# A recurrent mixer gated by a recursive top-2 expert network on one NeuronCore: a rewritten schedule

## The reference

```python
xn = layernorm(x)
# mixer: shifted input, six 128x128 projections, a scan along the sequence
xx = prev(xn) - xn
lin = lambda mix, W: (xn + xx * mix) @ W.T
r, alpha, g = sigmoid(lin(x_r, W_r)), sigmoid(lin(x_a, W_a)), sigmoid(lin(x_g, W_g))
decay = exp(-softplus(lin(x_w, W_w))); u = alpha * tanh(lin(x_k, W_k)) * lin(x_v, W_v)
state = state * decay + u                   # per time step
mixed = r * state
s = (group_norm(mixed, 16 groups of 8) * g) @ W_out.T + b_out
# experts: four rounds; round r routes with its own Wg, experts are shared
cur = xn
for r in range(4):
    cw = softmax over the top 2 of 4 logits of cur @ Wg[r] + bg[r]
    cur = cur + sum_e cw[e] * (gelu(cur @ W1[e] + b1[e]) @ W2[e] + b2[e])   # 128 -> 512 -> 128
out = x + s * silu(cur)
```

## Time and profile before

| | us |
|---|---|
| median of 3 runs | 847.47 (847.16 to 848.54) |
| the profiled execution | 848.68 |
| its span, first to last instruction | 846.8 |
| mean granted TensorE clock | 0.981 of full |

### The profile page before, as it was taken

How to read it: one execution, slowest core, us unless ns; L and a number is a source line. 1 busy time by engine, 2 the same in 40 slices (tenths; PEclk the granted TensorE clock), 3 DMA queues, 4 the chain that set the end, 5 groups by cost and what they waited for, 6 DMA issues and landing times.

```text
span 846.8 us, 10690 instructions
## 1 busy us (share of the span) xinstructions
PE 803.6 (95%) x3640; PEld 647.5 (76%) x3640; DVE 744.8 (88%) x1442; ACT 641.7 (76%) x882; POOL 158.4 (19%) x167
## 2 busy tenths in 40 slices
PE   3899999899999999999999999999999999999994
PEld 2678777677788887888878887788878888788883
DVE  7798879999999888988899888997989888998994
ACT  3578776677778787888778887788877887787872
POOL 6033522511111111111111111111111111011111
PEclk7799999999999999999999999999999999999997
DMA  7144423342364321543234432633316532264534
GB/s 221 51 88 100 90 49 87 88 87 39 88 150 100 88 50 32 144 101 87 50 82 96 99 91 36 150 95 76 63 31 148 121 94 50 42 178 105 138 63 87
DMA packets 40581, 76.94 MB, mean 91 GB/s; under 512 B 6480, under 2 KB 18896, under 8 KB 36432
## 3 DMA queue, kind: packets, MB, share of 16 engines
q0 software_dynamic: 18432, 33.56, 23.5%
q1 hardware_dynamic: 21808, 42.69, 16.0%
q10 hardware_dynamic: 288, 0.02, 0.0%
HBM read 40.34 MB, written 2.36 MB: 50 GB/s over the span
## 4 chain that ended last, share of the span: by engine, by line
PE 66%; DVE 20%; ACT 6%; DMA 4%; issue 3%; POOL 1%; SPq 0%; DVEq 0%; ACTq 0%; POOLq 0%
PE y_bank L822 10%; PE h_bank L778 10%; PE h_bank L777 10%; PE h_bank L776 10%; PE y_bank L818 10%; PE y_bank L817 10%; DVE g_lo L571 5%; ACT g L380 3%; ACT g_hi L384 2%; DMA cur<-tmp 2%; DVE tmp L582 2%; PE p_bank L776 1%; PE p_bank L778 1%; PE p_bank L777 1%; DVE xm L629 1%
## 5 line engine op out<-in xcount | busy, mean ns | idle before, releaser
L380 ACT ACTIVATE g<-h_bank,b_c 128x512 f32<-128x512 f32 x512 | 330.1, 683 | 83.1 <-PE h_bank L778 81.4
L571 DVE TENSOR_TENSOR g_lo<-g,g_hi 128x1024 fp32r<-128x1024 f32 x256 | 307.3, 1223 | 59.2 <-ACT g_hi L384 58.8
L384 ACT ACTIVATE g_hi<-g 128x1024 fp32r<-128x1024 f32 x256 | 272.2, 1063 | 8.1
L351 POOL DMA_DIRECT2D cur<-tmp x128 | 115.9, 905 | 671.3 <-DVE tmp L582 521.7
L776 PE MATMUL h_bank<-cur_lo,w_hi 128*128 128x512 f32 x512 | 206.8, 404 | 0.0
L778 PE MATMUL h_bank<-cur_hi,w_hi 128*128 128x512 f32 x512 | 204.2, 399 | 0.0
L777 PE MATMUL h_bank<-cur_hi,w_lo 128*128 128x512 f32 x512 | 203.9, 398 | 0.0
L817 PE MATMUL y_bank<-g_hi,w_hi 128*128 128x512 f32 x512 | 202.5, 396 | 0.0
L818 PE MATMUL y_bank<-g_hi,w_lo 128*128 128x512 f32 x512 | 202.2, 395 | 0.0
L822 PE MATMUL y_bank<-g_lo,w_hi 128*128 128x512 f32 x512 | 141.4, 397 | 2.9 <-DVE g_lo L571 2.9
L822 PEld LDWEIGHTS y_bank<-g_lo,w_hi 128*128 128x128 f32 x512 | 95.6, 188 | 28.0 <-DVE g_lo L571 5.5
(11 more groups left out here) (115 smaller groups left out, 571.6 us busy)
## 6 DMA issues: line engine op xcount, KB each, us to landing
cw_b<-cw_scratch SPq DMA_DIRECT2D x32, 1024.0 KB, 5.6
cur<-tmp POOLq DMA_DIRECT2D x128, 256.0 KB, 3.3
cur<-in_x SPq DMA_DIRECT2D x8, 256.0 KB, 5.3
xr<-in_x SPq DMA_DIRECT2D x8, 256.0 KB, 5.5
out<-o SPq DMA_DIRECT2D x8, 256.0 KB, 3.4
g<-in_w SPq DMA_DIRECT2D x4, 256.0 KB, 5.9
cw_scratch<-cw SPq DMA_DIRECT2D x32, 8.0 KB, 1.4
cw_b<-in_proj_t SPq DMA_DIRECT2D x1, 384.0 KB, 3.5
```

The costliest lines, as they stand in the source:

```text
L351: pool.dma_start(cur[:, s // E % NB * BLK:(s // E % NB + 1) * BLK], tmp[:, t % 2, :], accum_op=ALU.add).then_inc(summed, DMA)
L380: nc.scalar.activation(g[:, gb, ft * BLK:(ft + 1) * BLK], hb[ft][:, :], ACT.Gelu_apprx_tanh, bias=b1_c[:, e * FT + ft:e * FT + ft + 1]).th ...
L384: nc.scalar.activation(g_hi[:, gb, h], g[:, gb, h], ACT.Copy).then_inc(g_hi_done, 1)
L571: nc.vector.tensor_tensor(g_lo[:, gb, h], g[:, gb, h], as_f32(g_hi[:, gb, h]), ALU.subtract).then_inc(g_lo_done, 1)
```

## The change

The step order is now one loop over 128 steps on each engine. Its parts:
- Blocks are normed in groups (0 and 1; 2 and 3; 4 to 7). The scaling is done by ScalarE (`scale_block`), but for half of block 0. The turned block lies in p_bank (`turn_normed`), not r_bank; ScalarE (blocks 0 to 3) or VectorE (4 to 7) copies it to cur, and DMAs copy it on to xn_t.
- The low halves of the weights are made by VectorE, one expert at a time and between other work; GpSimd has only its DMAs. The weights' loads are in another order, in other buffers, and each expert is waited for by itself. Four small loads are issued by ScalarE.
- The routers work for 2, 2 and then 4 turns at a time; before it was one turn for each of the first eight, then four.
- The uses of p_bank have one count (`p_job`).
- The last two steps are added to cur by VectorE, and the last block is turned into two h banks and added and stored in halves.
- The end product is split into `end_scaled` and `end_product`.
- `down_done` is posted by the down products alone.

The diff, cut to its core:

```diff
+BATCHES = [(0, 2), (2, 2)] + [(k, QUADS) for k in range(QUADS, TURNS, QUADS)]
...
+NORM_GROUPS = [(0, 1), (2, 3), (4, 5, 6, 7)]
+NORM_SCALE = {2: 4, 3: 5, 4: 8, 5: 9, 6: 10, 7: 11}
+SPLIT_AT = {2: 5, 3: 6, 4: 9, 5: 10, 6: 11, 7: 12}
+SPLIT_AT.update({8: 25, 9: 25, 10: 27, 11: 27})
+SPLIT_AT.update({k: 4 * (k - 4) + (1 if k % 2 == 0 else -1) for k in range(12, TURNS)})
+LOGITS_AT = {0: 0, 1: 6, 2: 13}
+LOGITS_AT.update({n: 16 * n - 20 for n in range(3, len(BATCHES))})
+LATE = (0, 8, 16)
+
...
-            for e in range(E):
-                pool.wait_ge(hi_split, e + 1)
-                nc.gpsimd.tensor_tensor(w1_lo[:, e, :], w1_raw[:, e, :], as_f32(w1_hi[:, e, :]),
-                                        ALU.subtract).then_inc(lo_split, 1)
-            for e in range(E):
-                h = slice(e * FT, (e + 1) * FT)
-                pool.wait_ge(hi_split, E + e + 1)
...
+            for s in range(STEPS - ADDED_BY_DVE):
+                if s < E * NB and s % E == 0:
+                    pool.wait_ge(xn_copied, DMA * (s // E + 1))
+                pool.wait_ge(combined, s + 3)
+                if s > 0:
+                    pool.wait_ge(summed, DMA * s)
+                pool.dma_start(cur[:, block_of(s // E)], tmp[:, s % 2, :], accum_op=ALU.add).then_inc(summed, DMA)
...
+            def high_w1(e):
                 act.wait_ge(w1_loaded[e], DMA)
-                nc.scalar.activation(w1_hi[:, e, :], w1_raw[:, e, :], ACT.Copy).then_inc(hi_split, 1)
-
-            def router_tanh(k):
-                n, p = batch_of(k), slice(0, RP if k < NB else QUADS * RP)
+                nc.scalar.activation(w1_hi[:, e, :], w1_raw[:, e, :], ACT.Copy).then_inc(w1_high, 1)
...
+            def scale_block(b):
+
+                group = [b in blocks for blocks in NORM_GROUPS].index(True)
+                act.wait_ge(rstd_ready, group + 1)
+                if b >= 2:
+                    act.wait_ge(p_full, b - 1)
+                for t in range(TPB // 2 if b == 0 else 0, TPB):
+                    c = b * TPB + t
+                    last = nc.scalar.activation(xn_st[:, b % 2, t * D:(t + 1) * D], cur[:, c * D:(c + 1) * D],
+                                                ACT.Identity, bias=shift[:, c:c + 1], scale=rstd[:, c:c + 1])
+                last.then_inc(xn_ready, 1)
+
+            def store_block(b):
+
+                act.wait_ge(p_full, b + 1)
+                if b == 0:
+                    act.wait_ge(cur_split, 2)
+                nc.scalar.activation(cur[:, block_of(b)], pb[:, :], ACT.Copy).then_inc(p_empty, 1)
...
+            def hidden(s1, between=None):
+
+                e, gb = s1 % E, s1 % 2
+                if s1 > 0:
                     act.wait_ge(down_done, s1)
                 for half in range(2):
                     for ft in (2 * half, 2 * half + 1):
-                        act.wait_ge(up_done, 4 * s1 + ft + 1)
+                        act.wait_ge(up_done, FT * s1 + ft + 1)
...
+                if b == NB - 1:
+                    act.wait_ge(added, ADDED_BY_DVE)
+                else:
+                    act.wait_ge(summed, DMA * (STEPS - E * (NB - b - 1)))
...
+            high_w1(0)
+            high_w1(1)
+            high_w2(0)
+            high_w1(2)
+            scale_block(0)
+            scale_block(1)
+            high_w2(1)
+            high_w1(3)
+            high_w2(2)
+            store_block(0)
             act.wait_ge(small_loaded, DMA * SMALL)
-            hidden(0, 0, 0)
-            act.wait_ge(lo_split, 2 * E)
-            for i in range(PASSES):
-                one_pass(i)
+
+            def after_first_half():
+                store_block(1)
...
+                def between():
+                    for b in at_step(NORM_SCALE, s):
+                        scale_block(b)
+                    for n in at_step(LOGITS_AT, s - 2):
+                        if n >= 3:
+                            router_tanh(n)
+                    if s > END_FROM and (s - END_FROM) % E == 1:
+                        end_tanh((s - END_FROM) // E)
+
+                if s + 1 < STEPS:
+                    hidden(s + 1, between)
...
+            def low_w1(e):
+                dve.wait_ge(w1_high, e + 1)
+                nc.vector.tensor_tensor(w1_lo[:, e, :], w1_raw[:, e, :], as_f32(w1_hi[:, e, :]),
+                                        ALU.subtract).then_inc(w1_low, 1)
...
-                dve.wait_ge(down_done, s + 2)
...
+                dve.wait_ge(down_done, s + 1)
...
+                if s >= STEPS - ADDED_BY_DVE:
+                    last = cur[:, block_of(k)]
+                    dve.wait_ge(summed, DMA * (STEPS - ADDED_BY_DVE))
+                    dve.wait_ge(combined, s + 3)
+                    if s > STEPS - ADDED_BY_DVE:
+                        dve.wait_ge(added, s - STEPS + ADDED_BY_DVE)
+                    nc.vector.tensor_tensor(last, last, tmp[:, s % 2, :], ALU.add).then_inc(added, 1)
...
+            def end_scaled(b):
+
+                sx = xn_t[:, 2 * b:2 * b + 2, 1:LEN + 1]
+                dve.wait_ge(p_empty, p_job(2 * b + 1, J_S) + 1)
+                if b == NB - 1:
+                    dve.wait_ge(added, ADDED_BY_DVE)
+                else:
+                    dve.wait_ge(summed, DMA * (STEPS - E * (NB - b - 1)))
+                nc.vector.scalar_tensor_tensor(out=sx, in0=cur[:, block_of(b)].rearrange("p (b t) -> p b t", b=2),
+                                               scalar=0.5, in1=sx, op0=ALU.mult, op1=ALU.mult).then_inc(scaled, 1)
 
             def end_product(b):
+
+                t3 = th[:, b % 2, :].rearrange("p (b t) -> p b t", b=2)
+                dve.wait_ge(th_ready, b + 1)
+                dve.wait_ge(scaled, b + 1)
+                nc.vector.scalar_tensor_tensor(out=t3, in0=t3, scalar=1.0, in1=xn_t[:, 2 * b:2 * b + 2, 1:LEN + 1],
+                                               op0=ALU.add, op1=ALU.mult).then_inc(z_ready, 1)
+
+            def end_output(b):
...
+            for s in range(STEPS):
...
+                if s - 1 in (6, 13):
+                    router_scores({6: 1, 13: 2}[s - 1])
+                for m, stage in mixers_at(s):
+                    if stage == 0:
...
+                if s > END_FROM and (s - END_FROM) % E == 3:
+                    end_output((s - END_FROM) // E)
+                if s > END_FROM and (s - END_FROM) % E == 2:
+                    end_scaled((s - END_FROM) // E)
+                    end_product((s - END_FROM) // E)
+                for k in at_step(SPLIT_AT, s):
+                    if k >= NB:
                         split_cur(k)
+
...
+                        g_low_half(s + 1, half)
+                    if half == 0 and s in (0, 8, 15):
+                        router_gates({0: 0, 8: 1, 15: 2}[s])
...
+                for n in at_step(LOGITS_AT, s - 1):
+                    if n >= 3:
+                        router_scores(n)
+                for n in at_step(LOGITS_AT, s - 2):
+                    if n >= 3:
+                        router_gates(n)
+                if s - 1 in LATE:
+                    combine(s - 1)
+                if s not in LATE:
+                    combine(s)
...
+            for n in range(2):
+                h = slice(n * BLK // 2, (n + 1) * BLK // 2)
+                dve.wait_ge(half_turned, n + 1)
+                nc.vector.tensor_tensor(o[:, (NB - 1) % 2, h], hb[n][:, 0:BLK // 2], xr[:, (NB - 1) % 2, h],
+                                        ALU.add).then_inc(half_done, 1)
 
...
-            def turn(job, src, tiles, ready, count, first=False):
-
-                pe.wait_ge(ready, count)
-                if not first:
-                    pe.wait_ge(r_empty, job)
-                for t in range(tiles):
-                    ins = nc.tensor.transpose(rb[:, t * D:(t + 1) * D], src[:, t * D:(t + 1) * D], ident[:, :])
-                    if first and t == 0:
-                        ins.then_inc(down_done, 1)
...
+            def turn_normed(b):
+
+                if b == 0:
+                    pe.wait_ge(xn_first, 1)
+                else:
+                    pe.wait_ge(p_empty, b)
+                pe.wait_ge(xn_ready, b + 1)
+                for t in range(TPB):
+                    ins = nc.tensor.transpose(pb[:, t * D:(t + 1) * D], xn_st[:, b % 2, t * D:(t + 1) * D], ident[:, :])
+                ins.then_inc(p_full, 1)
+
...
+            def logits(n):
+
+                first, turns = BATCHES[n]
+                pe.wait_ge(r_empty, r_jobs["logits", n])
+                for i in range(turns):
+                    pe.wait_ge(cur_split, 2 * (first + i + 1))
+                    w = wg_pad[:, WG_AT - RP * i:WG_AT - RP * i + 128]
+                    q = (first + i) % SPLITS
+                    nc.tensor.matmul(rb[:, :], w, cur_lo[:, q, :], start=(i == 0), stop=False)
...
+            turn_normed(0)
+            up(0)
+            turn_normed(1)
+
+            for s in range(STEPS):
+                if s + 1 < STEPS:
+                    up(s + 1)
+                if s == 0:
```

(67 more changed lines are left out.)

720 lines of the change are left out of this document (319 added, 401 removed).

## The result

The kernel after takes 1099.59 us (median of four runs, 1097.42 to 1101.83), against 847.78 for the kernel before, measured beside it (also a median of four): a ratio of 1.297, with a 95% interval of 1.295 to 1.298. It is 252 us slower. The forecast was 1057, with a range that ended at 1095: right in sign and in the main cause, some 43 us short in size, and the measured time lies 5 us above the range. The profiled execution took 1097.42, its span is 1095.6, and its mean granted clock is 0.957 of full, where before had 0.981.

A forecast was written before the change was run, and what follows sets the result against it. TensorE was taken to bound the middle. The 846.8 us span, +174 for the wait, +51 for further terms, -9.5 at the start and -7 at the tail gave 1055.3; 1.5 more made 1057 us, range 1030 to 1095.

The forecast's parts named there:

- bare period: Mid-kernel step without extra work: 7.64 us against 6.27 on average before, +174 us over 127 periods.
- mixer stage 0: Mixer steps: VectorE's work and the project end at 2.6, costing 0.4 us each, 16 times, 6 us.
- six router gaps: Router steps: scores delay the next mixer work, 19 us, plus 7 us for the lower clock in five of them.
- ends of blocks, tanhs, logits, splits: Smaller middle terms: end_tanh 4.4, router tanh 1.5, end products 4.6, logits 2, split beside group norm 1.2 us.
- the forecast's +51: Middle: all costs on top of the bare 7.64 us steps, together +51 us, bounds 30 to 75.
- The wait: `hidden`: its uncorrected down_done wait now means the down product just ahead, so ScalarE's gelu starts only after it; +174 us.
- The start and the tail: Two ends: start -9.5 us without GpSimd's subtracts, first down product at 26.8; tail -7 us, 7.4 left.
- The routers: Six router steps: next mixer work comes later, costing 3.1, 2.9, 3.6, 3.1 and 6.7 us; stage 5 costs nothing.
- The norm's steps: Normed blocks: six `scale_block` at 0.9 us, 5.4 us; loads' order, xn_t by DMA and routers' grouping nothing to 3 us.
- The clock: Rival: a step's two idle stretches regularly lower the clock, 1105 us (one step in four) or 1247 (every step); chance 0.12.
- the rule of the Trainium skill that the prediction argued against: Kernel before: weight loads at 76% against VectorE's 88% would make VectorE the engine to watch; the prediction held TensorE bound.
- The rival of no slowdown: Rival: down(s) ends before ScalarE would begin, so the wait costs nothing and gains stay, 827 us; chance 0.04.

The follow-up runs named there:

- the mended kernel: The kernel after with hidden(s1) waiting for down_done >= s1 - 1 instead of s1: 844.32 us, ratio 0.996.
- the run with GpSimd busy: The mended kernel with eight 128x256 subtracts added on GpSimd, written to a buffer nobody reads: 848.14 us.
- the two other kernels with it mended throughout and no added work: The kernels called both mended (832.24 us) and the best version (828.08 us).
- the best version: The kernel called both mended, with block 3 split ahead of step 6's two low halves: 828.08 us, ratio 0.977.
- both mended: The mended kernel with blocks 4 to 7 turned one step later and step 110's end product ahead of the group norm: 832.24 us, ratio 0.982.

## Why the prediction was right in sign and short in size

The middle, as forecast and as measured in the kernel after:

| part of the 127 periods | forecast, us | measured, us |
|---|---|---|
| bare period x 127 | 7.64: 970.3 | 7.49: 951.2 |
| mixer stage 0, 16 times | 6 | 9.5 (0.65 each, one 0.32; one lies in a router's period) |
| six router gaps, their clock included | 26 | 30.4 |
| periods 2 to 12, above bare | 5.4 | 51.8 |
| period 18, above bare | 0 | 3.8 |
| ends of blocks, tanhs, logits, splits | 13.7 | 15.2 (the rest) |
| sum | 1021.4 | 1061.9 |

The second to sixth rows are the forecast's +51. They came to 110.7, above its upper bound of 75, and the largest part of that is one row.

**The wait: right.** The reading that `hidden` would wait for the product just ahead, and that ScalarE's lead of a hidden layer would be gone, is shown by the mended kernel and by the kernel before with the stronger wait. The period was 0.15 us too long in my sum: the gelu starts 0.43 behind the last down matmul, not 0.49, and the third gelu 2.27 behind the first (231.75 to 234.02), not 2.33, so up tile 2 starts at 3.42 instead of 3.56. That is 19 us the other way, and it hid part of the miss: by luck, the total is off by less than its terms.

**The start and the tail: right.** 26.8 forecast, 25.3 measured; 7.4 forecast, 8.4 measured. That GpSimd's subtracts had slowed the norm is confirmed by the run with GpSimd busy. In the mended kernel the start is 23.6: the first up product begins at nearly the same time there (13.36 against 13.50), but in the kernel after most of its matmuls stand at 0.43 us from each other, which accounts for nearly all of the 1.7. The wait has no part in this: the two other kernels with it mended throughout and no added work have 25.5 and 25.9.

**The routers: right in mechanism, 4 us short.** Periods 31, 47, 63, 79, 95 and 111 took 13.21, 12.15, 7.65, 12.91, 12.37 and 17.00. The one I had at nothing (63, whose mixer stage has no VectorE work) was 0.16 above bare. TensorE waits for the low half behind the scores, and the matmuls behind are at the lower level (timeline of TensorE, period 31):

```profile
312.16 0.58 PE L841 MATMUL p_bank<-xm_lo,pj_hi 128*128 128x256 f32 x1 [4.01 <-DVE xm_lo L661]
...
313.60 0.63 PE L841 MATMUL h_bank<-cur_lo,w_hi 128*128 128x512 f32 x1
314.03 0.63 PE L842 MATMUL h_bank<-cur_hi,w_lo 128*128 128x512 f32 x1
```

**The norm's steps: the step that failed.** I costed `scale_block` at 5.4 us, as ScalarE work between the halves of hidden, and wrote that the loads' order, xn_t by DMA and the routers' grouping "cost nothing to 3 us: ScalarE and VectorE have over 2 us of slack in a step of 7.64". The turns of the normed blocks, the early logits and the late combines had no term of their own. I counted the moved work by how long it takes and asked whether an engine had room for it. I didn't ask what TensorE has queued behind it. Periods 2 to 12 cost 51.8 us above bare, +46 on my term, which is more than the whole miss of the middle (40.5):
- the turns of normed blocks, periods 5, 6, 9, 10, 11 and 12 (11.89, 12.69, 11.88, 16.86, 16.95, 17.00): each stands on TensorE ahead of an up product and needs work that ScalarE or VectorE does inside the hidden layer after the down product. I had applied just this chain to the mixer's and the routers' work and not to `turn_normed`. Moving the turns took 21.6 us off periods 5 to 12; the clock below is part of this.
- the second group of logits in period 7 (14.80), which waits for the split of block 3 behind both g_lo. Moving the split took 3.6 us off in the mended order; in the kernel after it wasn't tried alone.
- the late combines in periods 2 and 10 (and 18): each holds a y bank until behind the low halves of the step whose down product wants it. Its size is shown for period 18 alone, 3.5 us; for the other two it wasn't tried, though with the turns moved the wait of period 10 for `combine(8)` shows, 2.50 us.
- `scale_block` itself: four tiles take 1.64 us, 0.41 each, above my upper bound of 1.4, and not 0.9. Six times that makes 10 us at most instead of 5.4.

**The clock.** The rival didn't come true: the pauses of a bare step (0.56 and 0.58 us in the one above; 0.87 and 0.52, or a single one of up to 1.30, in others) didn't bring it down, as the 70 periods of 7.49 show. But the clock cost more than I had for it. The kernel after has some 120 matmuls of 512 columns at 0.43 us from start to start, before had 18; at 0.195 us each (0.43 less 0.235) that is 24 us against 3.5, and I had 7. The granted clock by stretches (the columns are busy us of each engine, then the clock, the DMA share and GB/s):

```profile
25.00:190.00 165.00, 110.36 (x399) 82.21 (x398) 77.13 (x166) 79.64 (x122) 12.94 (x15) 0.84 0.23 58
190.00:862.00 672.00, 565.88 (x2384) 422.74 (x2385) 472.28 (x846) 409.88 (x576) 77.12 (x86) 0.98 0.30 69
```

Of the slow matmuls 58 lie in periods 2 to 12, behind the gaps of 4 to 8 us that I hadn't seen coming: some 11 us. The routers' periods have 35, some 6.8 us, which is the 7 that I had for them. The rest lie in the start (7), in period 18 (6) and in two periods with the end of a block, 103 and 107 (14). So most of the clock's excess is a consequence of the failed step and not a second cause. The 11 us are an estimate of its share of the 51.8: part of the slow matmuls may stand where TensorE would have waited anyway.

**The busy share.** By the rule of the Trainium skill that the prediction argued against (Perfetto Trace Analysis, Identifying the Most-Contended Engine: judge TensorE's headroom by the weight loads' busy share), 78% in the mended kernel would leave TensorE room. The trace doesn't agree: a bare step there takes 5.60 us, which is 24 matmuls at 0.233 back to back, and the best version shows matmuls at 97% with loads at 78%.

**The rival of no slowdown** had 827 for the order without the wait. The mended kernel took 844. That sum took 5 us off for stalls, though the text above it has the lost cover as a cost of "at most 5 us"; measured, the middle is 14.5 us longer than before's. It is the same mistake at half the size: periods 2 to 12 stand 25.3 us above bare in the mended kernel, 51.8 in the kernel after and 3.5 in the kernel before. With most of these stalls mended it is 828, and they are still 9.8 above bare.

What stays open: how the 46 us above my term, and the 27 us of interaction in these periods, divide over turns, logits, combines and clock.

## What to carry to other kernels

A semaphore whose first post is removed shifts every wait that counts it: look up each waiter, for a wait one item too strong computes the same result and costs, as here, 1.7 to 2 us in each of 127 steps. The sign of it in a profile is that no engine is near its limit and the largest wait occurs once a step. And when work is moved, ask not only whether its engine has room, but what the bounding engine has queued behind the consumer of that work: a wait of a few us there stops everything behind it, and here the clock added its part.

## What the runs showed of the hardware

- Four ScalarE instructions of 128x128 with a scale and a bias column took 1.64 us in a row, 0.41 apiece; one of 128x512 with a bias column took 0.68, and a pair of them started 0.59 apart. A quarter of the elements cost about 70% of the time. I had put it at 0.22.
- In the ordinary steps of 7.49 us of the kernel after, pauses such as 0.56 and 0.58 us, 0.87 and 0.52, or one of 1.30 (period 117), left the granted clock at its upper level, 2.4 GHz. Pauses of 4 to 9 us brought the lower one, 1.2 GHz, during them or right behind them, and 512-column matmuls then stood 0.43 us apart instead of 0.235. Between them it went either way, behind the very same pause too: 2.35 us ahead of down product 10 (up with both mended, low in the best version), and 1.68 and 1.67 ahead of the first up product (low in the kernel after, up in the mended one). It fell behind 1.92 in the kernel before and not behind 1.73 in the best version. In periods 103 and 107 of the kernel after it fell behind two short pauses, 1.30 and 0.96, and 1.57 and 0.44, with transposes or 256-column matmuls between them.
- VectorE and GpSimd hold each other up even when VectorE's instruction has 8 columns: 0.17 us alone, 0.58 to 0.71 beside 128x256 subtracts of 0.80, where every second one still took 0.17. Beside 128x512 subtracts of 1.23 in the kernel before, seven took 1.15 to 1.23 (one is in the earlier trace rows).
